# One barrier between layers, stores inside the last layer, and the causal mask on TensorE in a layered eight-layer model

## The reference, cut to what matters

```python
h = jnp.concatenate([_L0_tok_ref(x, ...), txt], axis=1)
h = h + _L0_attn_ref(_layernorm(h), ...)     # a state-space scan
h = h + _L0_ffn_ref(_layernorm(h), ...)      # experts
h = h + _L1_attn_ref(_layernorm(h), ...)
h = h + _L1_ffn_ref(_layernorm(h), ...)      # experts of attention
h = h + _L2_attn_ref(_layernorm(h), ...)
h = h + _L2_ffn_ref(_layernorm(h), ...)      # attention, then experts
h = h + _L3_attn_ref(_layernorm(h), ...)
h = h + _L3_ffn_ref(_layernorm(h), ...)      # experts
```

```python
causal = jnp.where(jnp.tril(jnp.ones((s, s), bool)), 0.0, -jnp.inf)   # _L1_ffn_ref
scores = jnp.einsum('bnesd,bntd->bnest', q, k) * d ** 0.5 + causal
att = jax.nn.softmax(scores, axis=-1)
qkv = jnp.einsum('bnest,bntd->bnesd', att, v)
```

```python
scores = jnp.einsum('bhqd,bhkd->bhqk', q, k) / math.sqrt(64)
int_scores = (jnp.abs(scores) * 1618.0).astype(jnp.int32)             # ttt_filter
scores = scores * jnp.where(int_scores % 3 == 0, 1 / PHI, 1.0)        # 0, 3 or 6 of mod 9
attn = jax.nn.softmax(scores, axis=-1)
attn = attn * (jnp.sin(C1 * attn) * jnp.exp(-attn ** 2 / PHI) + jnp.cos(C2 * attn))
ctx = jnp.einsum('bhqk,bhkd->bhqd', attn, v)                          # heads joined again
return ctx @ Wo + bo
```

## Time and profile before

| | us |
|---|---|
| median of 3 runs (lowest, highest) | 1405.03 (1403.05, 1408.33) |
| the profiled execution | 1410.15 |
| its span in the trace | 1408.4 |
| busy: PE, DVE, ACT, POOL | 911.6, 897.0, 502.0, 168.6 |

### The profile page before, as it was taken

One profiled execution on the slowest core, in us unless ns is written; L12 is line 12 of the kernel. 1 busy time (PEld: TensorE's weight loads), 2 busy tenths in 40 slices (PEclk: granted clock), 3 DMA queues, 4 the chain that ended last, 5 costly groups with the idle time before them and its releaser, 6 DMA issues. The chain is left out here.

```text
span 1408.4 us, 18770 instructions
## 1 busy us (share of the span) xinstructions
PE 911.6 (65%) x6784; PEld 603.8 (43%) x6784; DVE 897.0 (64%) x2008; ACT 502.0 (36%) x1064; POOL 168.6 (12%) x198
## 2 busy tenths in 40 slices
PE   3775796683767757365747866767546776745456
PEld 1244364552345235264523432646334542434444
DVE  6764554756545769976468544657545455898854
ACT  1632021151413157744235213023223130885512
POOL 0431001020410000000115200010114000000010
PEclk8885796885875887555769668888659577965558
DMA  6000000000000000000000000000000000000000
GB/s 201 1 1 1 0 1 1 1 2 0 1 1 1 1 1 1 1 1 1 0 5 0 1 1 0 1 1 2 1 1 1 1 1 1 1 1 1 1 1 5
DMA packets 3002, 8.61 MB, mean 6 GB/s; under 512 B 1589, under 2 KB 1589, under 8 KB 2717
## 3 DMA queue, kind: packets, MB, share of 16 engines
q1 hardware_dynamic: 2910, 7.41, 1.8%
HBM read 7.08 MB, written 0.34 MB: 5 GB/s over the span
## 5 line engine op out<-in xcount | busy, mean ns | idle before, releaser
L457 PE MATMUL banks<-p_embed,xn 82*64 82x82 f32 x112 | 21.1, 344 | 138.7 <-DVE xn L425 138.7
L2366 PE MATMUL banks<-attn_diag,attn_e 82*82 82x82 f32 x512 | 69.1, 316 | 40.2 <-DVE attn_z L2611 20.9
L2366 PEld LDWEIGHTS banks<-attn_diag,attn_e 82*82 82x82 f32 x512 | 63.8, 227 | 53.3 <-issue 29.9
L2380 PE MATMUL banks<-attn_frac,attn_vals 82*64 82x82 f32 x512 | 43.0, 350 | 60.6 <-DVE attn_frac L2646 60.6
L437 POOL TENSOR_TENSOR ffn_sums<-ffn_sums,neg_half 82x4 f32<-82x4 f32 x28 | 27.7, 1003 | 447.4 <-DVE ffn_sums L422 447.4
L457 PEld LDWEIGHTS banks<-p_embed,xn 82*64 82x64 f32 x112 | 12.7, 158 | 145.6 <-DVE xn L425 145.6
L1616 ACT ACTIVATE ffn_probs<-banks 82x984 f32<-82x984 f32 x40 | 37.3, 982 | 100.7 <-PE banks L1497 100.7
L537 POOL TENSOR_TENSOR mamba_drive<-mamba_spread_b,mamba_dtx 128x328 f32<-128x328 f32 x64 | 56.9, 898 | 70.8 <-DVE mamba_dtx L761 37.0
L2380 PEld LDWEIGHTS banks<-attn_frac,attn_vals 82*64 82x64 f32 x512 | 35.9, 224 | 68.3 <-DVE attn_frac L2646 34.8
L825 DVE TENSOR_TENSOR_SCAN mamba_state<-banks,mamba_drive 128x328 f32<-128x328 f32 x64 | 53.3, 832 | 14.1 <-issue 8.2
L1548 DVE TENSOR_REDUCE ffn_maxima<-banks 82x4 f32<-82x328 f32 x80 | 47.9, 660 | 14.1 <-PE banks L1516 14.1
(11 more groups left out here) (433 smaller groups left out, 2470.8 us busy)
## 6 DMA issues: line engine op xcount, KB each, us to landing
p_rest<-p_rest_dram SPq DMA_DIRECT2D x1, 2474.0 KB
low<-p_low_rest_dram SPq DMA_DIRECT2D x1, 1524.5 KB
patches<-p_patches_dram SPq DMA_DIRECT2D x3, 288.0 KB, 3.9
p_pairs<-p_pairs_dram SPq DMA_DIRECT2D x1, 514.0 KB
p_scan<-p_scan_dram SPq DMA_DIRECT2D x1, 419.5 KB
p_narrow_rest<-p_narrow_rest_dram SPq DMA_DIRECT2D x1, 381.0 KB
h<-p_text_dram SPq DMA_DIRECT2D x2, 164.0 KB
out_dram<-h SPq DMA_DIRECT2D x2, 164.0 KB
```

Of the source, the lines that this page charges most:

```text
L2366: last = pe.matmul(ps[4 + par][0:TP, (2 * c + t) * TP:(2 * c + t + 1) * TP], e[:, i, par, c, t * TP:(t + 1) * TP], diag[:, j % 2, 2 * par ...
L2380: last = pe.matmul(ps[6 + tile % 2][par * D:(par + 1) * D, 0:TP], vals[:, 2 * (tile // 2) + t, hd * D:(hd + 1) * D], frac[:, j % STEPS, pa ...
```

## The change

1. Seven layers keep the block's barrier and lose the clears and the second barrier behind it. A layer's semaphores live on until the next layer has begun, where SP's program clears them (`clear_old`). `begin`, `mamba` and `fold` keep `clear`.
2. The block of `store` is gone. In ffn3 SP issues one DMA for each group, 82 KB, as soon as the group's addition to `h` is done; in the last pass it then waits for all four. For that, `combine` adds group 0 after the sum of tile 4 (ahead of the product of tile 6) and group 1 at the end, in ffn0 too.
3. In the weights phase of ffn1 and ffn2 DVE's mask is gone. PE adds it to the scores: per half four matmuls (328 columns, bf16, stationary `maskQ`) behind the scores; ACT waits for them, and PE's values wait for ACT.
4. attn3: the factor 0.125 goes into the queries (a copy becomes a multiplication); the peaks are written negated; `shift` is gone, and ACT's exponentials wait for the peaks. In stage C `recip` of a step follows `copy_scaled` of the step before. `turn_out` of tiles 0 to 3 stands in the middle of round two's `turn_scaled`, that of tiles 4 to 7 after the last `weigh`; the bias of four tiles is one matmul of 256 columns. DVE adds four tiles after the first product of the last stage, four at the end.

```diff
 def layer_memory(nc, ctx, w, layer):
+    sems, held = [], ExitStack()
-        new = [ctx.enter_context(nc.semaphore(f"{layer}_{n}")) for n in names]
+        new = [held.enter_context(nc.semaphore(f"{layer}_{n}")) for n in names]
+def clear_old(sp, w):
+    for s in w.used_sems[1]:
+        sp.sem_clear(s)
...
 def combine(dve, w, gates, prod, y_ps, y_read, summed, h_ready, banks):
-    for g in range(GROUPS):
-        dve.wait_ge(summed, (g + 1) * U)
-        steps.did(dve.tensor_tensor(tiles(w.h, g), tiles(w.h, g), tiles(w.xn, g), ALU.add))
-    steps.wait(dve)
+        if i > U and (i - 1) % U == 0 or i == NT:
+            g = i // U - 1
+            dve.wait_ge(summed, (g + 1) * U)
+            dve.tensor_tensor(tiles(w.h, g), tiles(w.h, g), tiles(w.xn, g), ALU.add).then_inc(h_ready, 1)
+    dve.wait_ge(h_ready, GROUPS)
...
+            clear_old(sp, w)
+            for g in range(GROUPS):
+                sp.wait_ge(h_ready, g + 1)
+                at = (w.p * GROUPS + g) * G
+                sp.dma_start(w.out[at:at + G].rearrange("b (t q) n -> q (b t) n", t=2), tiles(w.h, g)).then_inc(w.stored, 16)
+            if w.p == PASSES - 1:
+                sp.wait_ge(w.stored, 16 * GROUPS * PASSES)
...
+    def pe_masked_scores(self, pe, h):
+        self.pe_scores(pe, h, True)
+        ident = self.w.ident_b[:, :].unsqueeze(1).unsqueeze(1).broadcast_to([128, 2, 2, TP])
+        for i in (2 * h, 2 * h + 1):
+            for j in range(2):
+                last = pe.matmul(self.diagonal(i, j), self.w.maskQ[:, :], ident, start=False, stop=True)
+            last.then_inc(self.s_ps, 1)
...
-            pe.wait_ge(self.masked, i + 1)
+            pe.wait_ge(self.probs_ready, i + 1)
...
-            dve.wait_ge(self.probs_ready, i + 1)
-            four = self.probs[:, i % 4, :, :].rearrange("p j (k c n) -> p (j k) c n", k=2, c=3)
-            for c in range(0, 3, 2):
-                last = dve.scalar_tensor_tensor(out=four[:, :, c, :], in0=four[:, :, c, :], scalar=2.0,
-                                                in1=each(self.w.causal01[:, 0:TP], 4), op0=ALU.min, op1=ALU.mult)
-            last.then_inc(self.masked, 1)
...
+            def turn_out(first, count, bank):
+                o = ps[bank][0:TP, 0:count * D].rearrange("p (i n) -> p i n", n=D)
+                pe.wait_ge(oT_ready, first + 1)
+                pe.matmul(o, w.ones_row[:, 0:TP], w.a3_bo[:, :].unsqueeze(1).broadcast_to([1, count, D]), start=True, stop=False)
                 for i in range(count):
+                    pe.wait_ge(oT_ready, first + i + 1)
+                    last = pe.matmul(o[:, i, :], oT[:, first + i, :], w.ident2[:, :], start=False, stop=(i == count - 1))
...
-                act.wait_ge(shift_ready, j + 1)
+                act.wait_ge(peak_ready, j + 1)
...
             for layer in LAYERS:
-                clear(layer(nc, d, w))
-            store(nc, w, out, stored)
+                new = layer(nc, d, w)
+                w.used_sems[0].close()
+                w.used_sems = new
```

More of the change, by code:

```diff
@@ L856, in mamba, with layer_memory @@
         return sems
-def layer_memory(nc, ctx, layer):
-    sems = []
+def layer_memory(nc, ctx, w, layer):
+    sems, held = [], ExitStack()
     def sb(name, shape, dt=F32):
@@ L931, in ffn0, with _ @@
         Y_BANKS = (4, 5, 6, 7)
+        @block.sync
+        def _(sp):
+            clear_old(sp, w)
         @block.gpsimd
@@ L1494, in pe_scores @@
                     if transposed and part == 0:
-                        last = pe.matmul(o[:, 0:SEQ], key[:, 0:TP], q, start=True, stop=True)
+                        pe.matmul(o[:, 0:SEQ], key[:, 0:TP], q, start=(k == 0), stop=False)
                     elif transposed:
-                        last = pe.matmul(o[:, SEQ:W3], key[:, TP:SEQ], q[:, TP:SEQ], start=True, stop=True)
+                        pe.matmul(o[:, SEQ:W3], key[:, TP:SEQ], q[:, TP:SEQ], start=False, stop=False)
                     elif part == 0:
@@ L1501, in pe_scores, with diagonal @@
                         pe.matmul(o[:, TP:W3], q[:, TP:SEQ], key, start=False, stop=False)
-                    if transposed and k == 1 and part == 1 and r % 2 == 1:
-                        last.then_inc(self.s_ps, 1)
+    def diagonal(self, i, j):
+        return self.w.psum[self.s_bank(i) + j][0:TP, 0:2 * self.W3].rearrange("p (k c n) -> p k c n", k=2, c=3)[:, :, 0:3:2, :]
+    def pe_masked_scores(self, pe, h):
[5 more added lines that the diff above has]
+            last.then_inc(self.s_ps, 1)
     def pe_maxima(self, pe):
-        W3 = self.W3
         for h in range(self.halves):
@@ L1512, in pe_maxima @@
                 for j in range(2):
-                    diagonal = self.w.psum[self.s_bank(2 * h + s) + j][0:TP, 0:2 * W3].rearrange(
-                        "p (k c n) -> p k c n", k=2, c=3)[:, :, 0:3:2, :]
                     mask = self.w.maskQ[:, :].unsqueeze(1).unsqueeze(1).broadcast_to([128, 2, 2, TP])
-                    last = pe.matmul(diagonal, self.w.ident_b[:, :], mask, start=False, stop=True)
+                    last = pe.matmul(self.diagonal(2 * h + s, j), self.w.ident_b[:, :], mask, start=False, stop=True)
                 last.then_inc(self.max_ps, 1)
@@ L2309, in attn3 @@
         ps = w.psum
-        EARLY = NT - 2
         def scores_of(j):
@@ L2462, in size @@
                     act.wait_ge(kept_ready, j - 1)
-                act.activation(mag[:, j % 2, :, :, :], scores_of(j), ACT.Abs, scale=1618.0 / 8.0).then_inc(mag_ready, 1)
+                act.activation(mag[:, j % 2, :, :, :], scores_of(j), ACT.Abs, scale=1618.0).then_inc(mag_ready, 1)
             def thirds(j):
@@ L2476, in exponentials @@
                 i = j % STEPS
-                act.wait_ge(shift_ready, j + 1)
+                act.wait_ge(peak_ready, j + 1)
                 for m in range(4):
                     head = e[:, i, m // 2, m % 2, :]
-                    last = act.activation(head, head, ACT.Exp, scale=0.125, bias=peak[:, i, m:m + 1],
+                    last = act.activation(head, head, ACT.Exp, bias=peak[:, i, m:m + 1],
                                           accum_out=total[:, i, m:m + 1])
@@ L2660, in _ @@
                     copy_scaled(t - 3)
-                shift(t)
                 if t >= 4:
@@ L2683, in _ @@
                     peaks(j)
-                    shift(j)
             for i in range(STEPS + 1):
```

83 lines of the change are left out of this document (34 added, 49 removed).

## The result

The changed kernel takes 1362.04 us (median of 4 runs, 1359.14 to 1363.82); the kernel before, 1404.04 (1397.07 to 1408.33). The ratio is 0.970, 95% interval 0.966 to 0.975. The profiled execution took 1360.61, with a span of 1358.7; against the profiled execution before that is 49.5 less, since that one was a long one and this a short one.

What follows compares the result with a forecast made beforehand. No engine was taken to bound the whole kernel; DVE is fullest in attn3 and all engines wait at the seams. The terms sum to -25.3 us, from 1405.03 to 1380, range 1365 to 1391.

Steps and rivals of the forecast that it cites:

- The seams: Between layers: removing second barriers and clears shortens the waits, -12.9 us in all (bounds -6 and -14).
- Rival D: Between layers: the next layer's first instruction costs what the second barrier hid; half the seam gain, 1386 us, chance 0.12.
- The store: Kernel's end: two groups' DMAs, the first issued while DVE still works, take 4.3 us instead of 7.9: -3.6.
- The end of attn3: The last weighing starts earlier, followed by one bias matmul and four turns: 5.2 us a pass, -10.4 for two.
- The shift: attn3: 32 small DVE instructions go at 0.1 us each, -3.2 (bounds -1 and -5).
- Stage C: attn3: reciprocal enters the DVE-PE chain, +1.4 us a pass, output turn on PE +0.8; +4.4 for two passes.
- The last additions: ffn0 and ffn3: an addition moves between the sums, only PE's waiting for banks may shorten: -0.6 us.
- The mask: Weights phases of ffn1 and ffn2: masking moves from DVE to PE, together +1 us (bounds -8 and +6).
- B: Rival: the clock rises to 1.00 in ffn1's early weights phase and ffn2's softmax; 1362 us, chance 0.08.
- C: Rival: the low clock spreads over ffn1's weights phase, steady halves take 5.8 us instead of 3.43; 1408 us, chance 0.04.

Runs made afterwards that it cites:

- e6: Kernel before with one barrier between layers and the semaphores cleared by SP in the next layer, nothing else; 1383.99 us, ratio 0.988.
- u1: Changed kernel with the clears and second barrier behind each of the seven layers put back; 1383.24 us, 0.984 of the kernel before.
- u3: Changed kernel with attn3's shift put back, as a multiplication of the peaks by -1; 1369.19 us, 0.974 of the kernel before.
- u4: Changed kernel with the reciprocal put back ahead of the copy in attn3's stage C; 1359.51 us, 0.968 of the kernel before.
- e9: Changed kernel with stage C's reciprocal ahead of the copy again and the first output turn moved behind round two's second weighing; 1356.66 us (one run).
- u2: Changed kernel with the causal mask of the weights phases put back from PE to DVE; 1372.47 us, 0.977 of the kernel before.
- e5: Kernel before with only the mask of ffn1's and ffn2's weights phases moved from DVE to PE; 1393.70 us, ratio 0.993.
- e10: Kernel of e9 with four idle matmuls behind each of the eight products of attn3's stage C; 1349.31 us, 0.962 of the kernel before.
- e12: Kernel of e10 with twelve idle matmuls at ffn1's start and four behind each of attn3's first seven last-stage weighings; 1348.35 us, 0.960 of the kernel before.
- e11: Kernel of e9 with twelve idle matmuls at the start of PE's programs in ffn1, ffn2 and attn3; 1354.41 us, 0.964 of the kernel before.

## Why the prediction was wrong, point by point

**The seams:** the wait was right, the worth wrong. 0.55 was to stay of each and 0.54 does; 0.8 was to stay between the passes and 0.8 does, and the waits together fell by 13.3 where 12.9 was forecast. But the -12.9 is -17.6 (e6) to -19.7 (u1) by the medians. The step that failed is the one that counted a shorter seam as nothing but a shorter wait, with the clock behind it as it was. In its place the traces show a full clock that comes earlier in attn3 (3.5 us a pass, u1) and, less surely, in ffn2 (1.0), and that comes later in ffn1's weights phase (1.4 the other way). Rival D, half of the gain, is refuted.

**The store:** -3.6 forecast, 7.86 to 4.08 = -3.8 seen. The estimate from the Trainium skill (page "DMA: Bandwidth & Descriptors", section "Anatomy of one DMA", its fixed 2.0 us) gave 3.2; that section is on DMAs issued from GpSimd, and these are issued from SP. The end here is 4.08 behind the last addition, nearer to the sum from rows. What decided was that the first group's packets were out of the way.

**The end of attn3:** -5.2 a pass. From DVE's first product of the last stage, which starts 2.67 earlier in pass 0 after the change, to the end of the last addition, which comes 8.2 earlier, 5.5 were gained. The paces were right: bias and turns took 1.14 and 1.38, overlapping, and from the bias's start to DVE's addition 2.48 passed (642.94 to 645.42), where 0.91 + 1.21 + 0.35 = 2.47 was forecast.

**The shift:** -3.2, and u3 shows -3.9. **Stage C:** +2.2 a pass; between the first and the last copy of stage C attn3 loses 2.0 in the traces, 1.2 for the reciprocal (u4) and 0.8 for the turn (e9 against u4). Both terms stand. **The last additions:** -0.6 forecast; beyond their seams the ffn0 and ffn3 that end in one got shorter by 0.3 together.

**The mask:** +1 forecast, -8.9 (u2) and -7.9 (e5) seen. Three sub-steps failed. A steady half was to take 3.44 and takes 3.25, because the values of a half, when nothing stands between them, take 0.98 and not 2 x 0.57. The masks at the low clock were to cost 1.1 in each of ffn1's first two halves, and the two together cost 1.1 (6.79 before, 7.86 after); ffn2 was to lose 1.3 and lost 0.4 (10.4 to 10.8). So ffn1's weights phase gained 2.1 where 0.8 was forecast. And the granted clock was to stay as in the earlier trace rows: it held beyond the phase and gave back 2.5 us a pass (42.7 to 40.2, without the seam), which no term had. That makes some -4.2 a pass. The Trainium skill, page "TensorEngine Tiling (Array Packing)", section "Key Properties", says that changing the tiling mode drains TensorE. The price that the forecast set beside it, 0.24 per half from the earlier trace rows, would have made the forecast worse: a steady half of 3.25 shows no pause of PE.

**The rivals.** B's figure, 1362, is the measured time, and that is luck, for its place was wrong: in the changed kernel ffn1's first two halves stayed at 0.55 to 0.58, and so did ffn2's weights phase (10.8 us, 0.56). The clock did rise, at attn3's start and behind ffn1's weights phase. What B priced did come in other traces: ffn1's second half at 1.00 in e5 and u1, and ffn2's weights phase at 1.00 in e9, pass 0, where ffn2 took 92.1 in place of 96.1. B is thus the right cause with the wrong sites and a chance of 0.08 that was far too low. C, the low clock spreading over ffn1's steady halves, was not seen.

**The sum again.** Seams as waits -13.3, store -3.8, attn3's end -11, shift -3.9, stage C +4.0 make -28.0, against the forecast's -25.7 for the same terms. With the mask at -8.9 and the clock behind the seams at 19.7 - 13.3, so -6.4, it is -43.3; 42.0 was measured. As both of these are differences of medians, known to some 8 us, the sum agrees better than it had to; that the two belong there rests on the layers in the traces.

## What to carry to other kernels

Where the granted clock is at 0.50 in a stretch, ask of each edit whether it changes PE's pauses ahead of it: removing the second barriers was worth by the medians a third to half as much again as the waits themselves, and in ffn1's weights phase the clock went the other way. A stretch in which another engine waits for PE at the low clock can be bought back with idle matmuls in PE's pauses (e10: 4.3 us of the 27 from stage C's first copy to its last), but where they do not fit into the pause at the low clock too, PE can fall behind first (e12, pass 0). And a forecast that holds the clock fixed should carry that as its widest bound.

## What was not expected of the hardware

The clock's course differs between executions of one and the same code. attn1 in pass 0 took 54.8 us at a granted clock of 0.86 in the changed kernel's profile, and 57.4 to 57.5 in those of u3, u4, e9, e10 and e11, whose programs up to there differ from it in nothing that computes; in u2 and e10 the same 54.8 came in pass 1. The 57.4 of e9, pass 0, were granted 0.81. ffn2 took 96.2 in one pass of e9 (granted 0.73) and 92.1 in the other (0.80). Such jumps of 2 to 4 us in single layers would account for runs of one kernel that spread by 4 to 16 us. They are why an edit of under 4 us shows in the layers of a trace rather than in the medians.
